# The last chunk of the second attention: sums on VectorE, tail in two halves

## The chip, the cores and the metric

One Trainium2 chip; the kernel runs on one of its cores. The metric is the device time of one execution in microseconds (us). Three timed runs of the kernel before took 1464.84, 1472.23 and 1472.28 us.

## The reference

Two layers on one sequence of 2048 rows and 128 columns. Each layer computes `x = x + s * silu(ffn(xn))`, with `xn` the layer norm of `x` and `s` an attention of `xn`. The change lies in the second layer's attention (16 heads of 64, causal), and in the last sum:

```python
scores = jnp.einsum('bqhd,bkhd->bhqk', q, k) / jnp.sqrt(jnp.float32(D_HEAD))
scores = jnp.where(causal, scores, jnp.float32(-jnp.inf))
pattern = jax.nn.softmax(scores, axis=-1)
z = jnp.einsum('bhqk,bkhd->bqhd', pattern, v)
attn_out = jnp.einsum('bqhd,hdm->bqm', z, W_O) + b_O
...
x = x + s * g
```

Everything is f32. `g`, the silu of the second layer's ffn, is ready before the second attention starts.

## The kernel before

The second attention (`attention1`) goes over 8 pairs of heads (NP = 8), 4 chunks of 512 query columns (NC = 4, C = 512, TC = 4 tiles of 128), and for chunk qc over the (qc+1)*4 tiles of 128 keys up to the diagonal. One (pair, chunk, key tile) is a step; there are 320 steps in 80 groups of 4. Chunks are numbered g = 0 to 31; chunk 31, pair 7 with queries 1536 to 2047, is the last, with 16 steps (304 to 319) in groups 76 to 79. Its last four steps are on the diagonal and have 512, 384, 256 and 128 query columns for each of the two heads.

For each step TensorE fills a unit of two psum banks with both heads' transposed scores (L1668, L1671), keys on partitions. There are three such units in a ring (RING = 3), and UNIT lists in order everything that passes through them: scores, projections, values, tiles for the row maxima, and mixings. A unit is refilled once its reader has freed it. ScalarE takes the exponential (`exponentials`, L1772) into one of six slots of `prob` (PR = 6). A slot is written again only when TensorE has weighed and the sum of six steps back has been added, for which ScalarE waits on `weighted` and `summed`. On the diagonal GpSimd sets the masked square of 128x256 to zero (`hide_later`, L1557); its four masks of a chunk stand in its queue ahead of the diagonal's adds. TensorE adds prob times values to `out_bank` (`weigh`, L1690), one group behind the scores.

The softmax's denominators are sums over keys. GpSimd adds the steps' prob tiles into `acc` (128 x 2 heads x 512), two buffers used in turn by chunk: the first two steps in one add (L1583), the others each with one add into `acc` (L1587), counted by `summed`. `total` (L1643) multiplies a matrix of ones with `acc`, so that each partition of `side_bank` gets its head's denominators. ScalarE copies `out_bank` to `z` (`copy_out`, L1779). VectorE in `scale` takes the reciprocal (L1850) and multiplies z by it (L1853). `mix` (L1652) multiplies z by the output weights, and `add_mixed` (L1859) adds this to `attn`, which holds the sum over the head pairs. For pair 7, `finish` then multiplies by g (L1808) and adds x (L1809), and SyncE (SP) stores the chunk's rows, 256 KB (L1544).

Each engine works through its own list in the order in which it is written; engines wait for each other by semaphores. VectorE's list is, group by group: the units of the group that it reads (maxima, turned maxima, mixings), then the scaling of a chunk that ended in the group before. Groups 76, 78 and 79 hold no unit for VectorE; group 77 holds the mixing of chunk 30, with its finish. On TensorE each group is: its units, the total of a chunk that ended a group ago, the group's four weighings. Behind group 79 come total 31, `scale(31)`, the mixing and the finish of chunk 31. `Chain` (L50) adds a semaphore step to an instruction and has VectorE wait for it, for an instruction that reads what the one before wrote.

Of the kernel before, what the change touches and what calls it, by code (L numbers as in the profile page):

```python
# [15 lines left out]
P = 128  # L16
S = 2048
D = 128
# [57 lines left out]
def prepare(nc, a, sh):  # L76

    with ExitStack() as ctx:
# [3 lines left out]
        def sem(name):  # L82
            return ctx.enter_context(nc.semaphore(name))
# [33 lines left out]
        parts_stored = sem("parts_stored")  # L117
        router_loaded = sem("router_loaded")
        logit_done = sem("logit_done")
        cs_done = sem("cs_done")  # L120

        pos_dram = a["L0_ffn_position_ids"][0]
        x_view = a["L0_attn_x"][0].rearrange("(t p) d -> p t d", p=P)
# [24 lines left out]
        @block.gpsimd  # L148
        def _(pool):
            nc.gpsimd.memset(sh.ident[:, :], 0.0).then_inc(ident_zero, 1)  # L150
            nc.gpsimd.memset(sh.ones[:, :], 1.0).then_inc(cs_done, 1)
            pool.wait_ge(ident_zero, 1)
            nc.gpsimd.affine_select(out=sh.ident[:, :], in_=sh.ident[:, :], compare_op=ALU.not_equal, fill=1.0,
                                    base=0, pattern=[[-1, P]], channel_multiplier=1).then_inc(ident_done, 1)

            pool.wait_ge(w_loaded, 16)
            for m in range(3):
                nc.gpsimd.tensor_copy(w_parts[:, m, :].rearrange("d (h j) -> d h j", j=HD0),
                                      wqkv[:, :].rearrange("d (h c j) -> d c h j", c=3, j=HD0)[:, m])\
                    .then_inc(w_parted, 1)  # L160
# [1238 lines left out]
def attention1(nc, a, sh, out):  # L1399

    with ExitStack() as ctx:
# [3 lines left out]
        def sem(name):  # L1405
            return ctx.enter_context(nc.semaphore(name))
# [12 lines left out]
        LAPS = GROUPS // NP  # L1419
        CHUNK_LAST = [s for s in range(STEPS) if STEP[s][2] == (STEP[s][1] + 1) * TC - 1]  # L1420
        ENDS = [s // PER for s in CHUNK_LAST]

        TILES = [("maximum", hp, (i, b)) for hp in range(NP) for i in range(T) for b in range(i // TC + 1)]
        MAXIMA = [8, 6, 6, 8, 8] + [(3, 5, 2, 5, 5, 2, 5, 5, 5, 3)[k % LAPS] for k in range(5, GROUPS - 5)] + [0] * 5
# [33 lines left out]

        BEFORE = [("project", 0, 0), ("project", 0, 1)] + TILES[0:TC] + [("value", 0, 0), ("turn", 0, 0)]
        LAST = [("mix", NP - 1, NC - 1)]  # L1460
        UNIT = BEFORE + [u for k in range(GROUPS) for u in rows_phase(k) + whole_phase(k)] + LAST
        AT = {u: n for n, u in enumerate(UNIT)}
        FREED = {}
# [35 lines left out]
        hidden_later = sem("hidden_later")  # L1499
        weighted = sem("weighted1")  # L1500
        summed = sem("summed")
        z_copied = sem("z_copied")
        totalled = sem("totalled")
        inv_done = sem("inv_done1")
# [34 lines left out]

        @block.sync  # L1540
        def _(sp):
            for c in range(NC):
                sp.wait_ge(result_done, c + 1)
                sp.dma_start(out[0].rearrange("(t p) d -> p t d", p=P)[:, c * TC:(c + 1) * TC, :],  # L1544
                             attn[:, c * TC:(c + 1) * TC, :]).then_inc(stored, 16)
            sp.wait_ge(stored, 16 * NC)

        @block.gpsimd
        def _(pool):
            nc.gpsimd.memset(neg_max[:, :, :, :], 0.0).then_inc(consts_set, 1)  # L1550

            def hide_later(s):
                hp, qc, kt = STEP[s]
                q0 = first_column(qc, kt)
                block = prob[:, s % PR, :, q0:q0 + P]
                pool.wait_ge(exp_done, s + 1)
                nc.gpsimd.affine_select(out=block, in_=block, compare_op=ALU.is_ge, fill=0.0, base=0,  # L1557
                                        pattern=[[0, 2], [1, P]], channel_multiplier=-1).then_inc(hidden_later, 1)

            for s, (hp, qc, kt) in enumerate(STEP):  # L1560
                g = hp * NC + qc
                q0 = first_column(qc, kt)
                sums = acc[:, g % 2, :, q0:C]
                if kt == qc * TC:

                    for later in range(s, s + TC):
                        hide_later(later)
                if kt >= qc * TC:
                    pool.wait_ge(hidden_later, g * TC + kt - qc * TC + 1)
                else:  # L1570
                    pool.wait_ge(exp_done, s + 1)
                if kt == 0 and qc:

                    pool.wait_ge(summed, s)
                    pool.sem_inc(summed, 1)
                    continue
                if kt <= 1 and g >= 2:

                    pool.wait_ge(totalled, g - 1)
                if kt == 0:  # L1580
                    nc.gpsimd.tensor_copy(sums, prob[:, s % PR, :, :]).then_inc(summed, 1)
                elif kt == 1 and qc:
                    nc.gpsimd.tensor_tensor(sums, prob[:, (s - 1) % PR, :, :], prob[:, s % PR, :, :], ALU.add)\  # L1583
                        .then_inc(summed, 1)
                else:
                    pool.wait_ge(summed, s)
                    nc.gpsimd.tensor_tensor(sums, sums, prob[:, s % PR, :, q0:C], ALU.add).then_inc(summed, 1)  # L1587

        @block.tensor
        def _(pe):  # L1590
# [42 lines left out]
                    .then_inc(unit_filled, 1)  # L1633

            def total(g):
                pe.wait_ge(summed, CHUNK_LAST[g] + 1)
                if g:

                    pe.wait_ge(inv_done, g)
                else:  # L1640
                    pe.wait_ge(bias_spread, 1)
                for m in range(2):
                    last = nc.tensor.matmul(side_bank[HALF[m], :], sh.ones[:, 0:W], acc[:, g % 2, m, :],  # L1643
                                            start=True, stop=True)
                last.then_inc(totalled, 1)

            def mix(hp, qc):
                to = room_for(("mix", hp, qc))
                g = hp * NC + qc
                pe.wait_ge(scaled, g + 1)  # L1650
                for j in range(TC):
                    last = nc.tensor.matmul(to[:, 0, j * P:(j + 1) * P], z[:, g % 2, j * P:(j + 1) * P],  # L1652
                                            wo[:, hp, :], start=True, stop=True)
                last.then_inc(unit_filled, 1)

            def scores(s):
                to = room_for(("scores", s, None))
# [80 lines left out]
        def _(act):  # L1738
# [24 lines left out]
            def exponentials(s):  # L1763
                hp, qc, kt = STEP[s]
                q0 = first_column(qc, kt)
                n = AT["scores", s, None]
                act.wait_ge(unit_filled, n + 1)
                if s >= PR:

                    act.wait_ge(weighted, s - PR + 1)  # L1770
                    act.wait_ge(summed, sums_of(s - PR))
                nc.scalar.activation(prob[:, s % PR, :, q0:C], unit_both[n % RING][:, :, q0:C], ACT.Exp, scale=SCALE)\  # L1772
                    .then_inc(exp_done, 1)

# [27 lines left out]
        def _(dve):  # L1802
# [45 lines left out]
            def scale(g):  # L1848
# [3 lines left out]
                dve.wait_ge(z_copied, g + 1)  # L1852
                nc.vector.tensor_tensor(z[:, g % 2, :], z[:, g % 2, :], inv[:, :], ALU.mult).then_inc(scaled, 1)  # L1853

            def add_mixed(hp, qc):
                n = AT["mix", hp, qc]
                tiles = slice(qc * TC, (qc + 1) * TC)
# [29 lines left out]
            for k in range(GROUPS):  # L1887
# [3 lines left out]
                    take(unit)  # L1891
                if k - 1 in ENDS:
                    scale(ENDS.index(k - 1))
            scale(NP * NC - 1)
            for unit in LAST:
                take(unit)


INPUTS = [
# [82 lines left out]
```

## Time and profile before

| | |
|---|---|
| timed runs, median of 3 | 1472.23 us (1464.84 to 1472.28) |
| profiled execution, its own time | 1467.72 us |
| its span | 1465.8 us, mean granted TensorE clock 0.966 |
| TensorE busy | 1340.9 us (91%) |
| VectorE busy | 1026.0 us (70%) |
| ScalarE busy | 731.0 us (50%) |
| GpSimd busy | 705.1 us (48%) |

The span goes from the first to the last instruction of the profiled execution, its own time is a little longer. PE is TensorE's matmul part, DVE VectorE, ACT ScalarE, POOL GpSimd, SP SyncE. Busy time of PE is modelled. PEclk is the granted clock, 1.00 for 2.4 GHz and 0.50 for 1.2 GHz. A row's L number is a line of the kernel; in the chain of waits a piece is the time for which the chain went through that instruction or queue, and "POOLq" is GpSimd's instruction queue. Where one row counts several instructions ("x4"), its time runs over all of them and its shape is that of the first. The tile `xa` in the rows is the buffer in which `attn` lies.

### The profile page before, as it was taken

To read this page: it belongs to the slowest core of one execution; us is meant where nothing else is said; L and a number is where in the kernel's file an instruction comes from. 1 tells how busy PE (TensorE), PEld (TensorE's weight loads), DVE (VectorE), ACT (ScalarE), POOL (GpSimd) and SP (SyncE) were. 2 spreads that over 40 slices of the span, in tenths; PEclk is the share of its full clock that TensorE was granted. 3 is DMA by queue.
4 is the path that set the end of the run, shared out by engine and by line. 5 is a ranking of instruction groups with operands and counts; after the bars stand their busy time and mean duration, and the time that the engine had idled before them with its cause. 6 is when DMAs were issued, how large, how long until landed. Compare 5 with 4: busy or idle time off the path is not lost.

```text
span 1465.8 us, 25676 instructions
## 1 busy us (share of the span) xinstructions
PE 1340.9 (91%) x9954; PEld 704.1 (48%) x9954; DVE 1026.0 (70%) x1612; ACT 731.0 (50%) x1167; POOL 705.1 (48%) x521
## 2 busy tenths in 40 slices
PE   4398899999999998889999999999999999999895
PEld 2288422222222226545555555555555555555552
DVE  5966588888888885686676676666666666766762
ACT  2034477787777786434434444444444344444341
POOL 0110106010010101257867777868678678687686
PEclk9599899999999999999999999999999999999997
DMA  4400131000000000000000000000000000000000
GB/s 151 142 28 1 48 113 39 2 1 2 1 2 2 1 2 1 1 0 1 1 1 1 1 1 1 1 1 1 1 1 1 1 1 1 1 1 1 8 8 14
DMA packets 18149, 21.56 MB, mean 15 GB/s; under 512 B 7640, under 2 KB 15856, under 8 KB 16496
## 3 DMA queue, kind: packets, MB, share of 16 engines
q1 hardware_dynamic: 18032, 19.94, 4.3%
q8 instruction: 81, 1.33, 0.4%
q14 instruction: 36, 0.29, 0.1%
HBM read 14.70 MB, written 5.24 MB: 14 GB/s over the span
## 4 chain that ended last, share of the span: by engine, by line
PE 41%; DVE 10%; ACT 3%; POOL 2%; issue 1%; POOLq 0%; ACTq 0%
PE psum L1690 12%; PE psum L1668 12%; PE psum L1620 4%; DVE part_max L1829 4%; DVE inv L1850 4%; PE psum L1671 3%; ACT prob L1772 2%; PE psum L1652 2%; PE psum L1607 2%; POOL acc L1587 2%; PE psum L1643 2%; PE psum L1598 1%; DVE z L1853 1%; PE psum L1600 1%; PE psum L1599 1%; PE psum L1625 1%
## 5 line engine op out<-in xcount | busy, mean ns | idle before, releaser
L1587 POOL TENSOR_TENSOR acc<-acc,prob 128x1024 f32<-128x1024 f32 (+3 forms) x264 | 523.5, 1983 | 89.7 <-ACT prob L1772 58.0
L1772 ACT ACTIVATE prob<-psum 128x1024 f32<-128x1024 f32 (+1 forms) x320 | 283.6, 898 | 355.3 <-PE psum L1671 347.8
L1829 DVE TENSOR_REDUCE part_max<-psum 128x2 f32<-128x1024 f32 (+2 forms) x320 | 336.9, 1064 | 171.9 <-PE psum L1620 87.2
L578 DVE TENSOR_SCALAR w<-psum 128x512 f32<-128x512 f32 x472 | 304.9, 686 | 59.1 <-PE psum L435 46.1
L529 ACT ACTIVATE w<-psum 128x512 f32<-128x512 f32 x552 | 293.7, 600 | 86.2 <-PE psum L435 86.1
L455 PE MATMUL psum<-w,v_cols 128*32 128x512 f32 x2048 | 274.6, 609 | 0.0
L1690 PE MATMUL psum<-prob,v_pair 128*64 128x512 f32 (+3 forms) x1280 | 251.9, 536 | 5.7 <-POOL prob L1557 5.7
L1668 PE MATMUL psum<-q_hi,k_hi 64*128 64x512 f32 (+3 forms) x640 | 139.1, 431 | 30.0 <-DVE part_max L1829 21.2
L1690 PEld LDWEIGHTS psum<-prob,v_pair 128*64 128x64 f32 x1280 | 88.2, 138 | 151.0 <-issue 135.7
L1620 PE MATMUL psum<-k_hi,q_hi 64*128 64x512 f32 (+3 forms) x640 | 133.2, 413 | 5.9 <-DVE part_max L1829 4.5
L1850 DVE RECIPROCAL inv<-psum 128x512 f32<-128x512 f32 x32 | 107.3, 3353 | 40.8 <-PE psum L1643 40.8
L1668 PE MATMUL psum<-q_lo,k_hi 64*128 64x512 f32 (+3 forms) x640 | 120.0, 370 | 0.0
L1668 PE MATMUL psum<-q_hi,k_lo 64*128 64x512 f32 (+3 forms) x640 | 119.8, 370 | 0.0
L1671 PE MATMUL psum<-max_rows,ones_r 64*128 64x512 f32 (+3 forms) x640 | 119.4, 369 | 0.0
L435 PEld LDWEIGHTS psum<-q_rows,k_rows 32*128 32x128 f32 x768 | 40.1, 181 | 153.8 <-ACT w L529 147.2
L279 POOL TENSOR_SCALAR xa<-xa,rstd_j,shift_j 128x128 f32<-128x128 f32 x16 | 7.0, 454 | 210.3 <-DVE shift_j L271 210.3
L435 PE MATMUL psum<-q_rows,k_rows 32*128 32x512 f32 x768 | 101.2, 493 | 0.1
L1620 PEld LDWEIGHTS psum<-k_hi,q_hi 64*128 64x128 f32 x640 | 61.9, 189 | 77.1 <-issue 40.8
L1668 PEld LDWEIGHTS psum<-q_hi,k_hi 64*128 64x128 f32 x640 | 61.6, 189 | 77.2 <-DVE part_max L1829 46.5
L1557 POOL TENSOR_SCALAR_AFFINE_SELECT prob<-prob 128x256 f32<-128x256 f32 x128 | 51.4, 410 | 88.6 <-ACT prob L1772 87.8
L1583 POOL TENSOR_TENSOR acc<-prob 128x1024 f32<-128x1024 f32 x24 | 57.2, 2383 | 44.3 <-ACT prob L1772 42.7
L455 PEld LDWEIGHTS psum<-w,v_cols 128*32 128x32 f32 x2048 | 40.6, 108 | 63.8 <-ACT w L529 53.0
(278 smaller groups left out, 1438.5 us busy)
## 6 DMA issues: line engine op xcount, KB each, us to landing
q_rows<-q_dram SPq DMA_DIRECT2D x12, 256.0 KB
k_rows<-k_dram SPq DMA_DIRECT2D x3, 1024.0 KB
q_dram<-parts SPq DMA_DIRECT2D x2, 1024.0 KB, 4.7
k_dram<-parts SPq DMA_DIRECT2D x2, 1024.0 KB, 7.8
x<-in_L_attn_x SPq DMA_DIRECT2D x4, 256.0 KB, 3.9
mask<-in_L_ffn_attention_mask SPq DMA_DIRECT2D x1, 1024.0 KB, 5.2
x_high<-q_dram SPq DMA_DIRECT2D x4, 256.0 KB
x_low<-k_dram SPq DMA_DIRECT2D x1, 1024.0 KB
```

The lines of the kernel that those rows point to most:

```text
L435: last = nc.tensor.matmul(pair_bank[n % RING][i], k_rows[group][rows, kt * P:(kt + 1) * P], q_rows[group][rows, qc * C:(qc + 1) * C], star ...
L455: last = nc.tensor.matmul(out_bank[turn % 2][h * VW:(h + 1) * VW, :], v_cols[group][:, kt, h, :], w[:, s % WR, h, :], start=(kt == 0), sto ...
L529: nc.scalar.activation(w[:, s % WR, 2 * m + i, :], pair_bank[n % RING][i], ACT.Relu)\
L578: nc.vector.tensor_scalar(w[:, s % WR, 2 * m + 1, :], pair_bank[n % RING][1], 0.0, None, ALU.max)\
L1587: nc.gpsimd.tensor_tensor(sums, sums, prob[:, s % PR, :, q0:C], ALU.add).then_inc(summed, 1)
L1620: last = nc.tensor.matmul(to[:, m, 0:n], q_hi[HALF[m], i * P:(i + 1) * P], k_hi[hp % 2][HALF[m], c * C:c * C + n], start=True, stop=not di ...
L1668: nc.tensor.matmul(to[:, m, q0:C], left[HALF[m], keys], right[HALF[m], at], start=n == 0, stop=False)
L1671: last = nc.tensor.matmul(to[:, m, q0:C], ones_r[HALF[m], :], max_rows[HALF[m], at], start=False, stop=True)
L1690: last = nc.tensor.matmul(out_bank[HALF[m], q0:C], v_pair[hp % 2][:, kt, HALF[m]], prob[:, s % PR, m, q0:C], start=kt == 0, stop=kt == (qc ...
L1772: nc.scalar.activation(prob[:, s % PR, :, q0:C], unit_both[n % RING][:, :, q0:C], ACT.Exp, scale=SCALE)\
L1829: nc.vector.tensor_reduce(part_max[:, :, i, c], unit_both[n % RING][:, :, 0:cols], AX_X, ALU.max)\
L1850: nc.vector.reciprocal(inv[:, :], side_bank).then_inc(inv_done, 1)
```

## The change

It concerns only chunk 31 (`FINAL`), whose steps begin at `FINAL_FIRST` = 304.

- GpSimd still sets the masks of the four diagonal steps, and adds nothing for this chunk. VectorE makes the 15 adds (`add_final`), each group's behind its other work of the group: 3, 4, 4 and 4 adds in groups 76 to 79. They count on a semaphore of their own, `final_summed`, for which TensorE's total 31 and ScalarE's exponentials wait.
- Ahead of group 79's adds VectorE multiplies the chunk's part of `attn` by g and adds x (`base_final`), over the 31 chunks mixed so far. Behind the last mixing only its product with g is then added.
- Reciprocal and scaling of z go in two halves of 256 columns (`scale_final`), the mixing in two halves of two tiles, each half into a bank of its own of the unit (`mix`), and the finishing of the result in two halves (`finish_final`): mixed times g into the buffer `inv`, then plus `attn`. SP stores 128 KB for each half.
- A semaphore that nothing waited for (`cs_done`) is gone.

The diff, with declarations left out:

```diff
@@ SyncE @@
+            out_view = out[0].rearrange("(t p) d -> p t d", p=P)
-            for c in range(NC):
+            for c in range(NC - 1):
                 sp.wait_ge(result_done, c + 1)
...
+            for part in range(HALVES):
+                at = slice(T - TC + part * TH, T - TC + (part + 1) * TH)
+                sp.wait_ge(result_done, NC + part)
+                sp.dma_start(out_view[:, at, :], attn[:, at, :]).then_inc(stored, 16)
+            sp.wait_ge(stored, 16 * (NC - 1 + HALVES))
@@ GpSimd, behind hide_later @@
+                if g == FINAL:
+                    continue
@@ TensorE @@
             def total(g):
-                pe.wait_ge(summed, CHUNK_LAST[g] + 1)
+                if g == FINAL:
+                    pe.wait_ge(final_summed, T - 1)
+                else:
+                    pe.wait_ge(summed, CHUNK_LAST[g] + 1)
...
                 for j in range(TC):
-                    last = nc.tensor.matmul(to[:, 0, j * P:(j + 1) * P], z[:, g % 2, j * P:(j + 1) * P],
-                                            wo[:, hp, :], start=True, stop=True)
-                last.then_inc(unit_filled, 1)
+                    if g == FINAL and j % TH == 0:
+                        pe.wait_ge(final_scaled, j // TH + 1)
+                    last = nc.tensor.matmul(to[:, j // TH if g == FINAL else 0, j * P:(j + 1) * P],
+                                            z[:, g % 2, j * P:(j + 1) * P], wo[:, hp, :], start=True, stop=True)
+                    if g == FINAL and j % TH == TH - 1:
+                        last.then_inc(final_mixed, 1)
+                if g != FINAL:
+                    last.then_inc(unit_filled, 1)
@@ ScalarE @@
                     act.wait_ge(weighted, s - PR + 1)
-                    act.wait_ge(summed, sums_of(s - PR))
+                    if s - PR >= FINAL_FIRST:
+                        act.wait_ge(final_summed, max(s - PR - FINAL_FIRST, 1))
+                    else:
+                        act.wait_ge(summed, sums_of(s - PR))
@@ VectorE @@
+            def add_final(s):
+                kt = s - FINAL_FIRST
+                q0 = first_column(NC - 1, kt)
+                sums = acc[:, FINAL % 2, :, q0:C]
+                if kt == 0:
+                    return
+                if kt >= (NC - 1) * TC:
+                    dve.wait_ge(hidden_later, FINAL * TC + kt - (NC - 1) * TC + 1)
+                else:
+                    dve.wait_ge(exp_done, s + 1)
+                if kt == 1:
+
+                    dve.wait_ge(totalled, FINAL - 1)
+                    nc.vector.tensor_tensor(sums, prob[:, (s - 1) % PR, :, :], prob[:, s % PR, :, :], ALU.add)\
+                        .then_inc(final_summed, 1)
+                else:
+                    dve.wait_ge(final_summed, kt - 1)
+                    nc.vector.tensor_tensor(sums, sums, prob[:, s % PR, :, q0:C], ALU.add).then_inc(final_summed, 1)
+
+            def base_final():
+                at = slice(T - TC, T)
+                dve.wait_ge(unit_freed[AT["mix", NP - 2, NC - 1] % RING], FREED["mix", NP - 2, NC - 1])
+                link(nc.vector.tensor_tensor(attn[:, at, :], attn[:, at, :], sh.g[:, at, :], ALU.mult))
+                link(nc.vector.tensor_tensor(attn[:, at, :], attn[:, at, :], sh.x[:, at, :], ALU.add))
+
+            def scale_final(part):
+                at = slice(part * TH * P, (part + 1) * TH * P)
+                if part == 0:
+                    dve.wait_ge(totalled, FINAL + 1)
+                    dve.wait_ge(z_copied, FINAL + 1)
+                link(nc.vector.reciprocal(inv[:, at], side_bank[:, at]))
+                nc.vector.tensor_tensor(z[:, FINAL % 2, at], z[:, FINAL % 2, at], inv[:, at], ALU.mult)\
+                    .then_inc(final_scaled, 1)
+
+            def finish_final(part):
+                tiles = slice(T - TC + part * TH, T - TC + (part + 1) * TH)
+                mixed = unit_both[AT["mix", NP - 1, NC - 1] % RING][:, part, part * TH * P:(part + 1) * TH * P]
+                product = inv[:, part * TH * P:(part + 1) * TH * P].rearrange("p (t d) -> p t d", d=D)
+                dve.wait_ge(final_mixed, part + 1)
+                dve.wait_ge(final_scaled, part + 1)
+                link(nc.vector.tensor_tensor(product, mixed.rearrange("p (t d) -> p t d", d=D), sh.g[:, tiles, :], ALU.mult))
+                nc.vector.tensor_tensor(attn[:, tiles, :], product, attn[:, tiles, :], ALU.add).then_inc(result_done, 1)
...
                 if k - 1 in ENDS:
                     scale(ENDS.index(k - 1))
-            scale(NP * NC - 1)
-            for unit in LAST:
-                take(unit)
+                if k == GROUPS - 1:
+                    base_final()
+                for s in range(k * PER, (k + 1) * PER):
+                    if s >= FINAL_FIRST:
+                        add_final(s)
+            scale_final(0)
+            scale_final(1)
+            finish_final(0)
+            finish_final(1)
```

## Rows read from the trace of the kernel before

**Rows 1.** Chain that ended last, 1416 to 1466: start us, us, what it went through.
```profile
1419.39 2.38 POOL acc L1587
...
1421.91 2.68 POOL acc L1587
...
1427.22 2.63 POOL acc L1587
...
1452.41 0.76 POOLq L1401
...
1453.21 1.43 PE psum L1643 x4
...
1454.66 3.37 DVE inv L1850
...
1458.06 0.70 DVE z L1853
...
1458.90 2.06 PE psum L1652 x8
...
1462.43 0.69 DVE xa L1809
```

**Rows 2.** Timeline of POOL, 1405 to 1466: start us, us, line, operation, count, idle.
```profile
1416.89 2.37 POOL L1583 TENSOR_TENSOR acc<-prob 128x1024 f32<-128x1024 f32 x1 [0.52 <-ACT prob L1772]
1419.39 25.79 POOL L1587 TENSOR_TENSOR acc<-acc,prob 128x1024 f32<-128x1024 f32 x10
1445.14 1.49 POOL L1557 TENSOR_SCALAR_AFFINE_SELECT prob<-prob 128x256 f32<-128x256 f32 x4
1446.59 6.56 POOL L1587 TENSOR_TENSOR acc<-acc,prob 128x1024 f32<-128x1024 f32 x4
```

**Rows 3.** Timeline of PE, 1424 to 1466.
```profile
1424.77 1.16 PE L1652 MATMUL psum<-wo,z 128*128 128x128 f32 x8
...
1439.64 0.28 PE L1671 MATMUL psum<-max_rows,ones_r 64*128 64x128 f32 x2
1445.60 4.54 PE L1690 MATMUL psum<-prob,v_pair 128*64 128x512 f32 x16 [5.68 <-POOL prob L1557]
```

**Rows 4.** Timeline of ACT, 1405 to 1466.
```profile
1430.68 3.81 ACT L1772 ACTIVATE prob<-psum 128x1024 f32<-128x1024 f32 x4 [4.77 <-PE psum L1671]
1438.18 2.54 ACT L1772 ACTIVATE prob<-psum 128x1024 f32<-128x1024 f32 x4 [3.69 <-PE psum L1671]
1450.18 0.59 ACT L1779 COPY z<-psum 128x512 f32<-128x512 f32 x1 [9.47 <-PE psum L1690]
```

**Rows 5.** Timeline of DVE, 1405 to 1466.
```profile
1417.55 3.36 DVE L1850 RECIPROCAL inv<-psum 128x512 f32<-128x512 f32 x1 [3.21 <-PE psum L1643]
1420.94 1.37 DVE L1853 TENSOR_TENSOR z<-z,inv 128x512 f32<-128x512 f32 x1
1425.96 0.69 DVE L1859 TENSOR_TENSOR xa<-psum,xa 128x512 f32<-128x512 f32 x1 [3.65 <-PE psum L1652]
...
1427.67 2.73 DVE L1809 TENSOR_TENSOR xa<-xa,x 128x512 f32<-128x512 f32 x1
```

**Rows 6.** DVE and POOL groups by shape, whole span: count, busy us, mean ns.
```profile
L1359 DVE TENSOR_TENSOR w_low<-w_heads,w_high 128x2048 fp32r<-128x2048 f32 x1 | 2.3, 2293 | 1.0 <-ACT w_high L1294 1.0
...
L308 DVE RECIPROCAL den<-den 128x16 f32<-128x16 f32 x16 | 4.1, 254 | 0.5
...
L1587 POOL TENSOR_TENSOR acc<-acc,prob 128x1024 f32<-128x1024 f32 x168 | 399.1, 2376 | 75.7 <-ACT prob L1772 58.0 <-POOL acc L1587 0.4
```

**Rows 7.** DMA issues by tensor: median us to landing.
```profile
out<-xa SPq DMA_DIRECT2D x4, 256.0 KB, 2.3
```

**Rows 8.** Windows of L1690, L1643, L1652: stretch, us, PE, PEld busy, PEclk, DMA.
```profile
1445.60:1450.20 4.60, 4.54 (x16) 1.72 (x16) 0.50 0.00 0
...
1416.40:1417.60 1.20, 1.08 (x4) 0.20 (x4) 1.00 0.02 7
...
1458.80:1461.00 2.20, 2.04 (x8) 1.78 (x8) 0.50 0.00 0
```

More of the change, by code:

```diff
@@ L119, in prepare @@
         logit_done = sem("logit_done")
-        cs_done = sem("cs_done")
         pos_dram = a["L0_ffn_position_ids"][0]
@@ L150, in _ @@
             nc.gpsimd.memset(sh.ident[:, :], 0.0).then_inc(ident_zero, 1)
-            nc.gpsimd.memset(sh.ones[:, :], 1.0).then_inc(cs_done, 1)
+            nc.gpsimd.memset(sh.ones[:, :], 1.0)
             pool.wait_ge(ident_zero, 1)
@@ L1421, in attention1 @@
         ENDS = [s // PER for s in CHUNK_LAST]
+        FINAL = NP * NC - 1
+        FINAL_FIRST = CHUNK_LAST[FINAL - 1] + 1
         TILES = [("maximum", hp, (i, b)) for hp in range(NP) for i in range(T) for b in range(i // TC + 1)]
@@ L1460, in attention1 @@
         LAST = [("mix", NP - 1, NC - 1)]
+        HALVES = 2
+        TH = TC // HALVES
         UNIT = BEFORE + [u for k in range(GROUPS) for u in rows_phase(k) + whole_phase(k)] + LAST
@@ L1501, in attention1 @@
         summed = sem("summed")
+        final_summed = sem("final_summed")
+        final_scaled = sem("final_scaled")
+        final_mixed = sem("final_mixed")
         z_copied = sem("z_copied")
@@ L1541, in _ @@
         def _(sp):
-            for c in range(NC):
+            out_view = out[0].rearrange("(t p) d -> p t d", p=P)
+            for c in range(NC - 1):
                 sp.wait_ge(result_done, c + 1)
-                sp.dma_start(out[0].rearrange("(t p) d -> p t d", p=P)[:, c * TC:(c + 1) * TC, :],
-                             attn[:, c * TC:(c + 1) * TC, :]).then_inc(stored, 16)
-            sp.wait_ge(stored, 16 * NC)
+                sp.dma_start(out_view[:, c * TC:(c + 1) * TC, :], attn[:, c * TC:(c + 1) * TC, :]).then_inc(stored, 16)
+            for part in range(HALVES):
[3 more added lines that the diff above has]
+            sp.wait_ge(stored, 16 * (NC - 1 + HALVES))
         @block.gpsimd
@@ L1649, in mix @@
                 g = hp * NC + qc
-                pe.wait_ge(scaled, g + 1)
+                if g != FINAL:
+                    pe.wait_ge(scaled, g + 1)
                 for j in range(TC):
-                    last = nc.tensor.matmul(to[:, 0, j * P:(j + 1) * P], z[:, g % 2, j * P:(j + 1) * P],
-                                            wo[:, hp, :], start=True, stop=True)
-                last.then_inc(unit_filled, 1)
+                    if g == FINAL and j % TH == 0:
[4 more added lines that the diff above has]
+                        last.then_inc(final_mixed, 1)
+                if g != FINAL:
+                    last.then_inc(unit_filled, 1)
             def scores(s):
```

## The prediction

> **What bounds the kernel now.** I read the chain that ended last first. In it GpSimd adds denominators from 1416.89 us, one add behind the other, until 1453.17 [rows 1, 2]: 15 adds, with nothing between them but the four masks at 1445.14 [rows 2]. Behind them stand the total on TensorE, the reciprocal, the scaling of z, the mixing and three VectorE operations, the last of which ends at 1463.12 [rows 1]; then comes a store that lands in 2.3 us [rows 7], to the span's end at 1465.8. The other engines are early: TensorE's last scores are out at 1439.92 and it then waits 5.68 us for a mask [rows 3]; ScalarE's last exponential ends at 1440.72 [rows 4]; VectorE has nothing to do from 1430.40 [rows 5] to the reciprocal at 1454.66. So the end is a GpSimd queue some 10 us behind TensorE, and then a string with nothing beside it. Up to 1416.4 the two kernels issue the same work in the same order.
>
> **Price of a VectorE add.** The trace has no VectorE add of 128x1024 f32 with both inputs in SBUF. The nearest rows: 0.69 us for 512 columns with GpSimd idle (the last row of rows 1), 2.29 us for 2048 [rows 6]. Between them a column costs (2293-693)/1536 = 1.04 ns, so 1024 cost 1.23, 768 0.96, 512 0.69, 256 0.43. With 0.03 between two dependent VectorE instructions (1454.66+3.37 to 1458.06, rows 1) a full add is 1.255. GpSimd takes 2.38 for the same add [rows 6]: my first upper bound. The second: beside GpSimd's adds, VectorE's 512 columns with two SBUF inputs took 1.37 and 2.73 [rows 5], 2 and 4 times as long. I take 1.23, since between 1416.4 and 1439.2 GpSimd now has nothing to do.
>
> **The sums, step by step.**
> - The total of chunk 30 and its reciprocal end at 1420.91 as now; z takes 0.69 instead of 1.37 [rows 5], since GpSimd rests: 1421.63.
> - Adds 1 to 3 (group 76): 3 x 1.255, to 1425.40. Queued behind them is the previous mixing's add, which starts at 1425.96 today because TensorE ends that mixing only at 1425.93 [rows 3, 5]; so it is not delayed, by 0.56 us. With its two finishing steps (the second takes 2.73 now, rows 5) it costs 3 x 0.72: 1428.09.
> - Adds 4 to 11 (groups 77, 78): 8 x 1.255, to 1438.13. The last one's exponential is done at 1434.5 [rows 4], 2.4 us before its turn.
> - The new base step (attn times g, then plus x, 2 x 0.72): 1439.57.
> - Group 79: four exponentials from 1438.18 to 1440.72 [rows 4]. GpSimd is free, so each mask (four in 1.49, rows 2) can follow its exponential, the first at about 1439.2. Adds of 1024, 768, 512 and 256 columns: 1.23+0.96+0.69+0.43 = 3.31. With masks hidden beside adds the sums end at 1439.7+3.31+0.1 = 1443.1; with masks and adds strictly in turn at 1439.57+1.49+3.31+0.2 = 1444.6.
>
> How much of the masks is paid? Today z was issued at 1420.94 while a GpSimd add ran until 1421.77, and ended at 1422.31; a finishing step issued at 1427.67 ended at 1430.40, the GpSimd add beside it at 1429.85 [rows 1, 5]. Both end 0.54 to 0.55 behind that GpSimd add, and the GpSimd add after the first is stretched to 2.68 from 2.38 [rows 1]. That is taking turns, not sharing. I take 1444.0, nearer the serial end. By the Trainium skill (SBUF — State Buffer, section SBUF: two separate sides), a VectorE operation with two SBUF inputs and a GpSimd one that reads SBUF exclude each other for the whole instruction, a rule that speaks against this change. By it alone the sums end at 1444.6, by bare durations at 1443.1; the trace agrees with it in the 1.37 and the 2.73 us.
>
> The end of the sums moves from 1453.17 to 1444.0: **9.2 us**. The four weighings (4.54 at clock 0.50, rows 8, so 2.3 at the full clock) follow the masks and end at about 1443.4, the copy of z (0.59, rows 4) at 1444.1, before the total is ready.
>
> **Who else waits for VectorE now.** An exponential waits for the sum six steps back. Tightest is the third of group 78, at 1430.68+1.9 = 1432.6 [rows 4], which needs add 4, done at 1429.35; the first of group 79 (1438.18) needs add 6, done at 1431.86. Both have over 3 us. The psum slot of the previous mixing is freed at 1426.65, as now. Were an add 2.38, add 3 would end at 1428.9 and the slot be free at 1429.6, about when TensorE starts group 78; only that group's third tile asks for it.
>
> **The tail.**
> - Total: 1.43 now [rows 1], 1.08 at the full clock [rows 8]. TensorE's granted clock was 0.50 in 1445.60 to 1450.20, behind 5.68 us of idling, and 1.00 at 1416.4 [rows 3, 8]. It now pauses under 1 us, so I take 1.15; the saving is 0.28, with bounds 0 and 0.35. It ends at 1444.1+1.15 = 1445.25.
> - Reciprocal in halves: 3.36 for 512 columns [rows 5], 0.254 for 16 [rows 6], so 6.25 ns a column and 1.755 for 256. z halves 0.43. The four instructions with gaps of 0.03 end at 1445.29+1.785+0.46+1.785+0.43 = 1449.75: 4.5 us behind the total against 4.12 now (1454.64 to 1458.76, rows 1), **0.38 lost**.
> - The first half's mixing lies beside the second reciprocal. The second half starts 0.14 behind z (as 1458.76 to 1458.90, rows 1) and takes half of 2.04, at clock 0.50 [rows 8], or half of 1.16 [rows 3]: TensorE will have waited for most of 4 us, so I take 1.02, to 1450.9. Meanwhile VectorE finishes half one (0.89, to 1450.67). Half two is 0.43+0.03+0.43 from 1450.95: **1451.85**. From z's end to the last operation's that is 2.1, against 4.36 now [rows 1]: 2.26 gained.
> - The store: 128 KB behind the last add, not 256 KB; SP issues the first half's 1.2 us before. I cost it at 0, with bounds of 0.3 either way for want of a row of this size (the 256 KB land in 2.3, rows 7). By an estimate from the skill's fit (DMA: Bandwidth & Descriptors, section Anatomy of one DMA), a fixed 2.0 us plus bytes over 436 GB/s, half the bytes would save 0.3 us.
>
> Sum: 9.2+0.28-0.38+2.26 = 11.3 us (1463.12 to 1451.85). From the profiled execution, span 1465.8 and time 1467.72, that gives 1454.5 and 1456.4. The timed runs have a median of 1472.23 (two at it, one at 1464.84), 4.5 above the profiled one: from there, 1460.9; from the mean of all four times, 1469.3, 1458.0. I name **1459**, between these. About 0.5% (7.3 us) is what a measurement of this kernel tells from no change; 11.3 is 0.77%.
>
> **Rivals.**
> - A, taking turns costs more: the masks of group 79 stand behind whole adds and the last waits on both ends. For it: the 2.73 us row; against it: only four masks, 1.5 us in all. Sums end at up to 1446, the gain is 9 to 10, time about 1461.
> - B, VectorE adds at GpSimd's rate, so nothing is won: 12 full ones plus 1536 columns are 13.5 full adds, 13.5 x 2.38 = 32.1 from 1421.63, with 3.6 of other work and 0.4 of masks: 1457.7. That is 4.5 later than now, and the tail gives back 2.1: 2.4 worse, about 1472 by the mean. Against it: 0.69 for 512 columns in both rows of a resting GpSimd.
> - C, slower: VectorE's adds are stretched by SBUF access, beyond the point where the sums end at 1455.3: (1455.3-1421.63-4.0)/13.5 = 2.2 us a full add. At the worst row's rate (4 times) they take 4.85 each, 65.5 in all, and the sums end at 1491: 36 us slower, 1505. Against it: this rate was seen only beside GpSimd's adds, and those are gone.
> - D, the gain is there but the runs' own spread of 7.4 us hides it: after near 1461, before near its 1464.84. The difference then is 0.3%.
> - E, TensorE is the true bound: its stream ends at 1439.92, then come exponentials, masks and weighing to about 1443.4. It takes nothing from the 9.2 as long as the masks come in time; if not, it is A.
>
> **How the numbers follow.** Forecast 0.74, A 0.09, B 0.04, C 0.03, D 0.10. Faster by over 0.5% holds the forecast and most of A, 0.82; the same holds D, B and a little of A, 0.14; slower holds C and the bad end of B, 0.04. The range: down to the lowest run less 11.3 and less another 2 (sums 0.9 earlier, mixing 0.4, total 0.1, store 0.3), 1464.84-13.3 = 1451; up to the highest run less 5, 1467, which takes in A and some of D.
>
> **What the profile after would show.** 12 full adds on VectorE at 1.23 us and three smaller; z of chunk 30 at 0.69; four masks between 1439.2 and 1443 with gaps; the total at about 1444.1; reciprocals of 1.76; the last VectorE operation at about 1452; a chain that runs on VectorE at the end. Full adds above 2.2 us would refute it, as would an exponential that waits for a VectorE add, or sums that end after 1447.

## The result, and the profile after

The changed kernel took 1452.28 us, median of 4 runs (1448.95 to 1454.69), against 1468.91 for the kernel before on the same chip (4 runs, 1464.84 to 1472.28): a ratio of 0.9886, 95% interval 0.9844 to 0.9929. It is faster by 16.6 us in the medians. The profiled executions differ by less: spans of 1465.8 and 1453.0, 12.8 us. Two later executions far above the rest, one of an experiment's kernel (1532.74 us, mean granted clock 0.84) and one of the kernel before (1835.12 us, 0.65), are in the medians below and not in the ratios.

To compare traces I count from the end of the total of chunk 30 (total 30), since the code up to there is the same. It is at 1417.50 before and at 1416.51 after. The column "predicted" holds the prediction's times less 1417.50.

| us behind total 30 | before | predicted | after |
|---|---|---|---|
| eleventh add ends | – | 20.6 | 21.05 |
| sums end | 35.67 | 26.5 | 26.50 |
| total 31 ends | 37.14 | 27.75 | 27.65 |
| z scaled | 41.26 | 32.25 | 32.01 |
| last VectorE operation ends | 45.62 | 34.35 | 34.21 |
| span ends | 48.3 | 37.0 | 36.5 |

The chain of waits of after, from a little ahead of the last chunk's first diagonal exponential on (start us, us, what it went through):

```profile
1432.44 3.58 PE psum L1711 x16
1436.02 0.90 PE psum L1689 x6
...
1437.19 1.04 ACT prob L1796
...
1438.29 0.88 POOL prob L1567
...
1439.24 1.36 DVE acc L1896
...
1440.69 0.98 DVE acc L1896
...
1441.77 0.71 DVE acc L1896
...
1442.58 0.43 DVE acc L1896
...
1443.06 1.10 PE psum L1658 x4
...
1444.18 1.77 DVE inv L1909
...
1448.58 1.24 PE psum L1670 x4
...
1450.30 0.42 DVE xa L1920
```

Before, this part of the chain was GpSimd's [rows 1]; its 15 adds are gone from it. VectorE's adds are there only from 1439.24 on, each behind the mask or the add in front. Ahead of them the chain runs on TensorE from total 30 on (weighings L1711, scores L1689) and through one exponential, which starts 20.68 us behind total 30 in both kernels: VectorE keeps up with the scores, and TensorE's stream is what now sets the start of the diagonal. After the sums come the tail's two reciprocals and the second half's mixing.

VectorE's timeline of after, against [rows 5]:

```profile
1416.55 3.36 DVE L1874 RECIPROCAL inv<-psum 128x512 f32<-128x512 f32 x1 [3.20 <-PE psum L1658]
1419.95 0.69 DVE L1877 TENSOR_TENSOR z<-z,inv 128x512 f32<-128x512 f32 x1
1420.56 1.22 DVE L1892 TENSOR_TENSOR acc<-prob 128x1024 f32<-128x1024 f32 x1
1421.88 2.55 DVE L1896 TENSOR_TENSOR acc<-acc,prob 128x1024 f32<-128x1024 f32 x2
1424.98 0.69 DVE L1926 TENSOR_TENSOR xa<-psum,xa 128x512 f32<-128x512 f32 x1 [0.55 <-PE psum L1670]
...
1427.04 10.52 DVE L1896 TENSOR_TENSOR acc<-acc,prob 128x1024 f32<-128x1024 f32 x8
1437.48 0.69 DVE L1901 TENSOR_TENSOR xa<-xa,g 128x512 f32<-128x512 f32 x1
1438.20 0.69 DVE L1902 TENSOR_TENSOR xa<-xa,x 128x512 f32<-128x512 f32 x1
1439.24 3.76 DVE L1896 TENSOR_TENSOR acc<-acc,prob 128x1024 f32<-128x1024 f32 x4 [0.35 <-POOL prob L1567]
...
1448.10 0.42 DVE L1910 TENSOR_TENSOR z<-z,inv 128x256 f32<-128x256 f32 x1
```

The full adds take 1.22 to 1.23; eight of them take 10.52, seven steps and one add of 1.23, so from one start to the next it is 1.33 (1.255 predicted). z takes 0.69, not 1.37, and the finish of chunk 30 two times 0.69. GpSimd of after, against [rows 2], and the DMA groups, against [rows 7]:

```profile
1408.18 7.19 POOL L1599 TENSOR_TENSOR acc<-acc,prob 128x1024 f32<-128x1024 f32 x4
1438.29 3.64 POOL L1567 TENSOR_SCALAR_AFFINE_SELECT prob<-prob 128x256 f32<-128x256 f32 x4 [22.92 <-ACT prob L1796]
```

```profile
out<-xa SPq DMA_DIRECT2D x3, 256.0 KB, 2.3
...
out<-xa SPq DMA_DIRECT2D x2, 128.0 KB, 1.8
```

The masks no longer stand behind GpSimd's adds: the first starts at 1438.29, 21.78 behind total 30 and 22.92 after GpSimd's last work, where before it started 27.64 behind. They take 3.64 in all, not 1.49. And 128 KB land in 1.8 us where 256 KB take 2.3.

### The profile page after: what moved, and what is told of

The parts are those of the page before. It is cut to its first block, busy times and chain, and to the rows that moved or that the text cites. A ratio compares the mean times of both kernels' runs of the same rounds, so it can differ in the third digit from the quotient of the medians.

```text
span 1453.0 us, 25683 instructions
## 1 busy us (share of the span) xinstructions
PE 1337.5 (92%) x9954; PEld 702.8 (48%) x9954; DVE 1040.5 (72%) x1632; ACT 730.6 (50%) x1167; POOL 673.8 (46%) x506
## 3 DMA queue, kind: packets, MB, share of 16 engines
q8 instruction: 81, 1.33, 0.4%
## 4 chain that ended last, share of the span: by engine, by line
PE 41%; DVE 10%; ACT 3%; issue 1%; POOL 1%; DVEq 0%; POOLq 0%; ACTq 0%
PE psum L1711 13%; PE psum L1689 12%; DVE part_max L1853 4%; PE psum L1632 4%; DVE inv L1874 3%; PE psum L1692 3%; ACT prob L1796 3%; PE psum L1670 2%; PE psum L1619 2%; PE psum L1658 2%; PE psum L1610 1%; DVE z L1877 1%; PE psum L1612 1%; PE psum L1611 1%; PE psum L1637 1%
## 5 line engine op out<-in xcount | busy, mean ns | idle before, releaser
L1599 POOL TENSOR_TENSOR acc<-acc,prob 128x1024 f32<-128x1024 f32 (+3 forms) x250 | 492.6, 1970 | 87.6 <-ACT prob L1796 57.8
L1711 PE MATMUL psum<-prob,v_pair 128*64 128x512 f32 (+3 forms) x1280 | 250.2, 532 | 0.7 <-POOL prob L1567 0.7
L1689 PE MATMUL psum<-q_hi,k_hi 64*128 64x512 f32 (+3 forms) x640 | 139.1, 431 | 30.9 <-DVE part_max L1853 21.6
L1711 PEld LDWEIGHTS psum<-prob,v_pair 128*64 128x64 f32 x1280 | 87.4, 137 | 145.3 <-issue 134.3
L1689 PE MATMUL psum<-q_lo,k_hi 64*128 64x512 f32 (+3 forms) x640 | 119.2, 368 | 0.0
L1689 PE MATMUL psum<-q_hi,k_lo 64*128 64x512 f32 (+3 forms) x640 | 119.1, 368 | 0.0
L1874 DVE RECIPROCAL inv<-psum 128x512 f32<-128x512 f32 x31 | 103.9, 3352 | 16.5 <-PE psum L1658 16.5
L1689 PEld LDWEIGHTS psum<-q_hi,k_hi 64*128 64x128 f32 x640 | 61.5, 188 | 78.7 <-DVE part_max L1853 47.4
```

The costliest lines, as they stand in the source:

```text
L1689: nc.tensor.matmul(to[:, m, q0:C], left[HALF[m], keys], right[HALF[m], at], start=n == 0, stop=False)
L1711: last = nc.tensor.matmul(out_bank[HALF[m], q0:C], v_pair[hp % 2][:, kt, HALF[m]], prob[:, s % PR, m, q0:C], start=kt == 0, stop=kt == (qc ...
L1874: nc.vector.reciprocal(inv[:, :], side_bank).then_inc(inv_done, 1)
```

## Experiments

All ratios are against the kernel before on the same chip. "Behind total 30" is as above; "in after" is the first trace of the changed kernel.

**Which part carries the gain.** The adds alone: no base step, the old tail, the store whole.

```diff
-                if k == GROUPS - 1:
-                    base_final()
...
-            scale_final(0)
-            scale_final(1)
-            finish_final(0)
-            finish_final(1)
+            scale(NP * NC - 1)
+            for unit in LAST:
+                take(unit)
```

> VectorE makes the last chunk's 15 adds; reciprocal, scaling, mixing, finishing and store are whole, as in the kernel before, and there is no base step. All offsets are from the end of total 30 on TensorE, which is 1417.50 us in the trace of before (sums end 35.7 later, last VectorE operation 45.6 later) and 1416.51 in that of after (26.5 and 34.2 later). My theory, the term 'sums 9.2 us': sums end at 26.0 to 26.6, last VectorE operation at 35.7 to 36.1, so the time falls by 9 to 10 us against before (ratio 0.993 to 0.994). Rival, that the halves and the base step carry the gain: the time falls by under 3 us.

Measured: 1453.23 us (7 runs), ratio 0.992 (0.9891 to 0.9949). VectorE's timeline:

```profile
1411.22 3.36 DVE L1864 RECIPROCAL inv<-psum 128x512 f32<-128x512 f32 x1 [3.20 <-PE psum L1654]
...
1433.39 1.23 DVE L1886 TENSOR_TENSOR acc<-acc,prob 128x1024 f32<-128x1024 f32 x1 [1.17 <-POOL prob L1563]
1434.92 2.48 DVE L1886 TENSOR_TENSOR acc<-acc,prob 128x768 f32<-128x768 f32 x3 [0.30 <-POOL prob L1563]
1438.58 3.36 DVE L1864 RECIPROCAL inv<-psum 128x512 f32<-128x512 f32 x1 [1.18 <-PE psum L1654]
...
1446.35 0.69 DVE L1823 TENSOR_TENSOR xa<-xa,x 128x512 f32<-128x512 f32 x1
```

Total 30 ends at 1411.17. The sums end at 1437.40, 26.2 behind it, the last VectorE operation at 1447.04, 35.9: both inside what was expected, 9.75 us sooner than before. The ratio is a little under the expected 0.993 to 0.994, which its interval holds. The adds carry the gain.

The other half, with GpSimd adding as before:

```diff
-                if g == FINAL:
-                    continue
...
-                for s in range(k * PER, (k + 1) * PER):
-                    if s >= FINAL_FIRST:
-                        add_final(s)
```

> GpSimd adds as in the kernel before; only the base step ahead, the halves of reciprocal, scaling, mixing and finishing, and the two stores are taken from the change. My theory, the term 'tail 2.2 us': sums still end 35.5 to 35.9 us behind total 30, the last VectorE operation 43.3 to 43.6 behind it (45.6 in before), the store lands 0.0 to 0.4 sooner behind that: 2.0 to 2.7 us in all, ratio 0.998, too little to be told in the time. Rival: the base step beside GpSimd's adds delays these (it takes turns with them) and the sums end 1 us or more later, so that half of the gain is gone.

Measured: 1461.36 us (12 runs), ratio 0.9989 (0.9964 to 1.0013), no difference by the time. The trace's total 30 ends at 1411.21. GpSimd's timeline, then VectorE's:

```profile
1413.10 26.31 POOL L1597 TENSOR_TENSOR acc<-acc,prob 128x1024 f32<-128x1024 f32 x10
...
1440.81 6.57 POOL L1597 TENSOR_TENSOR acc<-acc,prob 128x1024 f32<-128x1024 f32 x4
```

```profile
1424.03 2.89 DVE L1893 TENSOR_TENSOR xa<-xa,g 128x512 f32<-128x512 f32 x1
1426.95 2.74 DVE L1894 TENSOR_TENSOR xa<-xa,x 128x512 f32<-128x512 f32 x1
...
1454.73 0.43 DVE L1912 TENSOR_TENSOR xa<-inv,xa 128x256 f32<-128x256 f32 x1
```

The sums end at 1447.38, 36.2 behind total 30: 0.5 later than before, because the base step's two operations stood beside GpSimd's adds (2.89 and 2.74 us, and the ten adds 26.31 instead of 25.79, rows 2). The last VectorE operation is at 1455.16, 43.95 behind: 1.7 gained. Neither theory's numbers held (at most 35.9 and 43.6 in the first, 1 or more in the rival), and both mechanisms are there: the tail itself gains 2.2 (7.78 from the sums' end instead of 9.95), and the base step takes 0.5 of it. In the whole change GpSimd adds nothing for this chunk, and the base step still costs 0.3, by the masks: the sums end 26.5 behind total 30 in after and 26.2 with the adds alone. GpSimd of the adds alone:

```profile
1432.95 0.41 POOL L1563 TENSOR_SCALAR_AFFINE_SELECT prob<-prob 128x256 f32<-128x256 f32 x1 [22.91 <-ACT prob L1786]
```

The first mask starts 21.78 behind total 30 in both. Here nothing runs beside it and it takes 0.41; in after it starts while the base step's second operation runs (1438.20 to 1438.89), takes 0.86, and VectorE's first diagonal add starts 22.7 behind total 30 instead of 22.2. So the halves and the base step add 1.66 to the 9.75 of the adds (35.87 to 34.21). The two ratios multiply to 0.9909.

> The changed kernel again, beside before on one chip. The traces account for 11.4 us between total 30 and the last VectorE operation and 0.4 in the store; the first comparison's medians differ by 16.6 us. Theory 'the rest is the spread of the runs': ratio 0.991 to 0.993 (10 to 13 us). Rival 'the change saves another 4 to 5 us further up': ratio 0.988 to 0.989 again, and in the trace total 30 ends 4 to 5 us sooner than in that of before.

Measured: 1453.66 us (6 runs), ratio 0.991 (0.9879 to 0.9941). The theory's ratio came. Sums end 26.50, last VectorE operation 34.2 behind total 30, as in the first trace of after; total 30 ends at 1417.32, as late as in before's, so the rival's 4 to 5 us further up are not there. Where the spread of the medians comes from is below.

**What a GpSimd instruction beside VectorE costs.** GpSimd gets five adds beside VectorE's:

```diff
                 if g == FINAL:
+                    if 1 <= kt <= 5:
+                        pool.wait_ge(totalled, FINAL)
+                        pool.wait_ge(pool_beside, kt - 1)
+                        other = acc[:, 1 - FINAL % 2, :, :]
+                        nc.gpsimd.tensor_tensor(other, other, other, ALU.add).then_inc(pool_beside, 1)
                     continue
```

> The changed kernel with GpSimd kept at work beside VectorE's adds: five adds of 128x1024 f32 that read and write the buffer of the chunk before, whose sums nobody needs any more, from the end of total 30 on. Theory 'taking turns': a VectorE add issued beside one of them waits for its end, so about five VectorE adds take 3.4 to 3.7 us instead of 1.23, GpSimd's stretch from 2.38 to up to 3.6, and the eleventh add ends 9 to 12 us later than in after; the whole is at best level with before. Rival 'they share the bandwidth': adds of 1.4 to 2.5 us side by side, the eleventh add at most 6 us later.

Measured: 1461.48 us (10 runs), ratio 0.9986 (0.9966 to 1.0007). Single instructions of GpSimd and of VectorE, beside each other:

```profile
1412.10 1.89 POOL L1584 TENSOR_TENSOR acc<-acc 128x1024 f32<-128x1024 f32 x1 [1.23 <-PE psum L1664]
...
1418.48 2.69 POOL L1584 TENSOR_TENSOR acc<-acc 128x1024 f32<-128x1024 f32 x1
...
1421.31 2.69 POOL L1584 TENSOR_TENSOR acc<-acc 128x1024 f32<-128x1024 f32 x1
```

```profile
1416.51 2.91 DVE L1898 TENSOR_TENSOR acc<-prob 128x1024 f32<-128x1024 f32 x1
...
1419.52 2.73 DVE L1902 TENSOR_TENSOR acc<-acc,prob 128x1024 f32<-128x1024 f32 x1
...
1422.36 2.73 DVE L1902 TENSOR_TENSOR acc<-acc,prob 128x1024 f32<-128x1024 f32 x1
```

The first GpSimd add lay beside the reciprocal, which reads psum, and took 1.89: with one tensor as both inputs an add is cheaper than the 2.38 of [rows 6], which I had reckoned with. The last two took 2.69. VectorE's three beside them took 2.91, 2.73 and 2.73 instead of 1.22. GpSimd's last two end at 1421.17 and 1424.00, and VectorE's last two 1.08 and 1.09 behind them, at 1422.25 and 1425.09. That is what comes out if each VectorE add gets its turn about 0.15 before the GpSimd add's recorded end and then takes its usual 1.22, and if the next GpSimd add is longer by what it waits. From one start to the next it is 2.83 for both, near 1.89+1.22 less twice that 0.15. These are turns, not shares.

The price was sized wrongly, though: the eleventh add ends 25.6 behind total 30, 4.5 us later than in after, not 9 to 12, because the first of the five had no VectorE operation with two SBUF inputs beside it, the second only z, and an add alone is shorter than I had it. The size by itself would fit the rival (at most 6); the ends of the instructions don't. The last VectorE operation comes 39.5 behind total 30, 5.3 later than in after. The timed runs are level with before, though by the trace this kernel should be 6.6 us faster (its span ends 41.7 behind total 30, before's 48.3); the section on the medians takes this up. The rule of the Trainium skill that the prediction weighed (SBUF — State Buffer, section SBUF: two separate sides) agrees with these rows, except that by them the turn passes about 0.15 before the recorded end.

The masks then, left out in the last chunk:

```diff
                 pool.wait_ge(exp_done, s + 1)
+                if s >= FINAL_FIRST:
+                    pool.sem_inc(hidden_later, 1)
+                    return
```

> The changed kernel without GpSimd's masks in the last chunk, so the keys behind the diagonal of the last 512 queries count too (that part of the computation is changed); the counts of the masks are raised as soon as the exponential is done. Theory: the masks' turns cost what I took over the bare durations, 0.9 us: sums end at 25.3 to 25.9 us behind total 30 (26.5 in after). Rival: masks hidden beside adds, cost only the first one's wait of 0.35 us: 26.1 to 26.5.

Measured: one run, 1450.16 us; sums end 26.05 behind total 30. The masks cost 0.45 us, between the two theories (0.6 to 1.2, and 0 to 0.4). In after, masks and adds do take turns, but it is the masks that wait: beside VectorE's operations three of the four last 0.86, 1.38 and 1.12 us, and the one that does not, 0.40. VectorE only waits 0.35 for the first mask and 0.1 inside its first add (1.35).

**The tail's clock.** Matmuls that nobody reads, in TensorE's pauses:

```diff
                     if g == FINAL and j % TH == 0:
+                        for _ in range(2 - j // TH):
+                            for m in range(2):
+                                nc.tensor.matmul(out_bank[HALF[m], :], sh.ones[:, 0:W], acc[:, g % 2, m, :],
+                                                 start=True, stop=True)
```

> The changed kernel with idle-time matmuls on TensorE whose results nobody reads: two pairs between total 31 and the first half's mixing, one pair between the halves. Theory 'the second mixing costs 1.22 us since the clock has fallen': it takes 0.6 to 0.7 instead, VectorE's last half begins 0.4 to 0.5 sooner, last VectorE operation 33.7 to 33.8 us behind total 30 (34.2 in after). Rival: the 1.22 has another cause, nothing moves.

Measured: one run, 1449.31 us. The mixing's windows, first of after, then of this kernel (stretch, us, busy PE and PEld, granted clock, DMA):

```profile
1446.50:1447.40 0.90, 0.79 (x4) 0.52 (x4) 0.77 0.00 0
1448.50:1449.90 1.40, 1.22 (x4) 0.93 (x4) 0.50 0.00 0
```

```profile
1441.50:1442.30 0.80, 0.71 (x4) 0.52 (x4) 1.00 0.00 0
1443.70:1444.50 0.80, 0.71 (x4) 0.52 (x4) 1.00 0.00 0
```

At the granted clock of 1.00 the second half takes 0.71, not 1.22. VectorE begins its last half without a wait, and the last operation ends 33.7 behind total 30: 0.5 us gained, as expected.

**Another tail.** What is left on the path is mostly the two reciprocals of 1.76 each, over denominators that stand 64 times in psum. With queries on partitions there are 8 columns to invert:

```diff
+            def total_tile(j):
+                pe.wait_ge(final_summed, (NC - 1) * TC + j)
...
+                    last = nc.tensor.matmul(side_bank[:, 2 * j + m:2 * j + m + 1], acc[:, FINAL % 2, m, j * P:(j + 1) * P],
+                                            sh.ones[:, 0:1], start=True, stop=True)
...
+                nc.vector.reciprocal(inv_q[:, :], side_bank[:, 0:2 * TC]).then_inc(final_scaled, 1)
...
+                    nc.vector.scalar_tensor_tensor(out=inv[:, at], in0=half_bank(j // TH)[:, 1, at],
+                                                   scalar=inv_q[:, 2 * j + 1:2 * j + 2],
+                                                   in1=z[:, 1 - FINAL % 2, at], op0=ALU.mult, op1=ALU.add)\
```

> The changed kernel with another tail for the last chunk: the denominators are brought query by row (acc as weights, one column of ones moving, a tile as soon as its last add is done), so the reciprocal is of 8 columns, not of 512; z is mixed unscaled, one matmul per head and tile, beside the last adds' totals; ScalarE scales head 0, VectorE scales head 1 and adds (4 operations of 128 columns), then times g and plus the base in halves. Theory, the reciprocals of 2 x 1.76 us are most of what is left on the path: last VectorE operation 31 to 32 us behind total 30 (34.2 in after), 2 to 3 us gained. Rival: small operations (8 matmuls of one column, 8 scalings) cost as much as they replace: 33.5 to 35, no gain.

Measured: 1454.93 us (6 runs), ratio 0.9919 (0.9887 to 0.9952). VectorE's timeline and the mixing's window:

```profile
1435.00 3.76 DVE L1924 TENSOR_TENSOR acc<-acc,prob 128x1024 f32<-128x1024 f32 x4 [0.36 <-POOL prob L1573]
1439.73 0.21 DVE L1934 RECIPROCAL inv_q<-psum 128x8 f32<-128x8 f32 x1 [0.97 <-PE psum L1673]
1441.35 0.61 DVE L1943 SCALAR_TENSOR_TENSOR inv<-psum,inv_q,z 128x128 f32<-128x128 f32 x2 [1.41 <-ACT z L1849]
...
1443.89 0.42 DVE L1950 TENSOR_TENSOR xa<-inv,xa 128x256 f32<-128x256 f32 x1
```

```profile
1439.60:1441.60 2.00, 1.98 (x16) 1.69 (x16) 0.54 0.00 0
```

The reciprocal takes 0.21. The sums still end 26.5 behind total 30 (1412.27), the last operation 32.05: 2.2 us sooner than in after, just outside the expected 31 to 32. That is less than the timed runs can tell: their ratio of 0.9919 is no better than the changed kernel's 0.991 beside it. The mixing took 1.98 at a clock of 0.54. To keep the clock:

```diff
+                n = (C, C // 2, 0, C // 2)[j]
+                for m in range(2 if n else 0):
+                    nc.tensor.matmul(half_bank(0)[HALF[m], 0, 0:n], sh.ones[:, 0:W], acc[:, 1 - FINAL % 2, m, 0:n],
+                                     start=True, stop=True)
```

> The tail by row, with three pairs of matmuls on TensorE whose results nobody reads (512, 256 and 256 columns) behind the totals of tiles 0, 1 and 3. Theory: in the tail by row the last mixing took 1.98 us since the granted clock had fallen to 0.50 before it; with TensorE kept at work it takes 1.0 to 1.3, and the last VectorE operation is 31.0 to 31.5 us behind the end of total 30 (32.04 in the tail by row, 34.2 in after). In time it would be 2.7 to 3.2 us better than after, 0.2%, less than the comparison can tell. Rival: the added matmuls stand in the way of the masks' weighings and totals, and the sums' totals end later: 32 or more.

Measured: 1453.64 us (6 runs), ratio 0.9924 (0.9898 to 0.9949). The mixing's window:

```profile
1450.70:1452.00 1.30, 1.16 (x16) 0.97 (x16) 1.00 0.00 0
```

Its clock is 1.00 and it takes 1.16 as the theory had it, but it begins 29.2 us behind total 30 instead of 27.35, behind the added matmuls, and the last operation is at 33.5. The rival was right: 1.5 us worse than without them.

**The rest of the medians' difference.**

> The changed kernel once more, beside the tail kept at work. The extra 4 to 5 us of the first comparison's medians over the 11.8 us of the traces: if they are the spread of the part in front of total 30, whose code is the same, the ratio against before is 0.990 to 0.993 and total 30 ends anywhere between 1411 and 1418 us whatever the kernel. If the change saved them, the ratio is at or under 0.989 and total 30 ends sooner than in any trace of before.

Measured: 1450.49 us (6 runs), ratio 0.9926 (0.9897 to 0.9954), as the theory of the spread had it; total 30 ends at 1411.53, sums and last operation 26.5 and 34.2 behind it. Windows of TensorE in before and in this run, long ahead of the change (stretch, us, busy PE, granted clock, DMA):

```profile
130.00:180.00 50.00, 40.39 (x260) 0.80 0.10 32
600.00:620.00 20.00, 17.10 (x132) 0.91 0.00 1
725.00:745.00 20.00, 18.12 (x120) 0.91 0.00 1
```

```profile
130.00:180.00 50.00, 40.38 (x289) 0.86 0.11 34
600.00:620.00 20.00, 16.60 (x144) 1.00 0.00 1
725.00:745.00 20.00, 18.03 (x139) 1.00 0.00 1
```

In the first trace the clock is at 0.50 for a part of each of these windows, in the other it is so only in the first, and for less of it. Added up from the clock records of all eleven traces, the time at 0.50 ahead of 1405 us goes with the place of total 30:

| at 0.50 ahead of 1405 us | total 30 ends | traces |
|---|---|---|
| 68.3 us | 1411.2 to 1412.3 | seven: the changed kernel's third, the adds alone, the halves alone, GpSimd's five adds, no masks, TensorE's pauses filled, the tail by row |
| 78.5 us | 1416.5 | the changed kernel's first |
| 81.9 us | 1417.3 and 1417.5 | the changed kernel's second, before |
| 92.2 us | 1421.5 | the tail kept at work |

So up to 10 us of a run lie in how long the clock is at 1.2 GHz ahead of the change, whatever the kernel. The latest place, 1421.5, is outside the expected 1411 to 1418, and it is that of a changed kernel. Why it differs between executions of the same code, no run here shows.

The timed runs have their spans on record. Less what their kernel's trace has behind total 30 (48.3 before, 36.5 after, 41.7 with GpSimd's five adds), they give an estimate of where total 30 ended. Of 41 runs of before in the three later comparisons, 27 come to 1411 to 1413, 3 to 1414 to 1415, 9 to 1417 to 1418 and 2 to 1422 to 1424; of the changed kernel's 16, 9 to 1411 to 1413, 6 to 1416 to 1418 and 1 to 1423. The levels are the same in both kernels, and a median of a few runs depends on how many fall on which. An interval over so few runs can miss that: of the ten runs with GpSimd's five adds eight come to 1417 or later, which accounts for their being level with before.

## Why the prediction was right

- **Bound and mechanism**: as put. The chain went through GpSimd's adds and now does not; with them alone on VectorE 9.75 of 11.4 us are there.
- **Price of an add**: 1.23 between rows of 512 and 2048 columns; measured 1.22 to 1.23. The gap of 0.03 was too small: between these adds, each of which waits on two semaphores, it is 0.10, and the eleventh add ends 0.4 us late. That the second wait is the reason is not shown.
- **The masks**: 0.9 us taken over the bare durations, of which they cost 0.45; the wider gaps between the adds made up the other 0.4. The sums' end at 26.5 is right to a tenth, but by two errors that cancel, which is luck. The rule of turns held, and the step that went wrong is who waits: mostly the masks, which had room.
- **The base step**: taken as 1.44 of VectorE's time and nothing more. It also lengthened the first mask from 0.41 to 0.86.
- **Who else waits**: no exponential waited for a VectorE add, and the previous mixing's add started 0.55 us after the third add, as worked out (0.56).
- **Tail**: total 1.08 to 1.10 (1.15 taken); reciprocals and scalings 4.36 from the total (4.5); second mixing 1.22 at clock 0.50 (1.02 taken from halving 2.04; a half costs more than half, 0.71 at clock 1.00 where the whole takes 1.16); from z to the last operation 2.20 (2.1). In all 34.2 against 34.35.
- **Store**: costed at 0 with bounds of 0.3; it gained 0.47, outside them (2.24 from the last operation to the span's end instead of 2.71). The Trainium skill's fit (DMA: Bandwidth & Descriptors, section Anatomy of one DMA) gave 0.3; the page states it for DMAs that GpSimd issues, and this store is issued by SyncE. By the rows 128 KB less save 0.5 of landing, and both landings lie under the estimates by that fit (1.8 and 2.3 against 2.3 and 2.6).
- **The number**: 1459 named, 1452.28 measured, inside the range of 1451 to 1467. Of the 6.7 us between them 0.6 is the gain (11.3 forecast, 11.9 in the traces: 11.41 to the last VectorE operation and 0.47 in the store) and 1.4 the starting level, 1459+11.3 against a median of 1468.91. The other 4.7 are what the first comparison's medians show over the traces. By their spans the changed kernel's four runs have total 30 at 1410.6, 1411.5 and twice 1416.5. Before's four have only times; less the 2 us by which a run's time mostly exceeds its span they come to about 1414.5, 1415.3 and twice 1422, later by 4.7 on average and on places that total 30 also takes in other runs. That the early clock put it there is what the traces suggest; but for after's first, these runs have no trace, so it isn't shown for them. The three comparisons gave 0.9886, 0.991 and 0.9926 (medians 16.6, 9.7 and 12.4 us apart); 11.9 us is 0.9919, inside all three intervals.
- **Rivals**: A (dearer turns), B and C fell: the sums end at 26.5, not at A's 28.5 (1446), and an add takes 1.22 us, against 2.2 from which on the change would lose. D fell as well: the slowest run of after lies 10 us under the fastest of before. E is true as far as it went: TensorE's stream now leads up to the first diagonal exponential, and as the prediction said that took nothing from the gain. C is what the five added GpSimd adds show on a small scale: three VectorE adds that had to wait, and what followed from them, took back 5.3 us.

## What to carry to other kernels

Here GpSimd was 10 us behind TensorE at the end of the kernel and VectorE had been idle for 24, so moving the last queue of work paid: the sums end 9.2 us sooner. VectorE now waits for the first mask, behind TensorE's stream, so adds that are faster still could win little more. VectorE's operations with two SBUF inputs took turns with GpSimd's adds and masks (2.73 instead of 1.22 us for an add), so such a move pays most if GpSimd then rests; a few short masks may stay, as long as they and not VectorE do the waiting. An operation put beside the first mask to fill a pause cost 0.3 us. In a tail of single steps, ask of each reciprocal how many of its columns are different numbers: 8 columns cost 0.21 us where 512 cost 3.36.

## What was not expected of the hardware

- Parts of the trace far ahead of the change, with the same code, ran at a granted clock of 0.50 for different lengths of time, and moved everything behind by 6 to 10 us.
- A GpSimd add of 128x1024 with one tensor as both inputs takes 1.89 us, with two different ones 2.38.
- Where VectorE and GpSimd took turns, the turn passed about 0.15 us before the recorded end of the instruction that had it.
- Filling TensorE's pauses kept the clock at 1.00 both times, and helped (0.5 us) only where the filling stood in front of nothing.
